# LSTM gates with the batch on the partitions in a merged stage: states as stationary operand in four column groups, weights moving, and a new order of the small work around them

## The reference, cut to what matters

```python
x = x + _L1_ffn_ref(_L1_cond2_ref(x, cond_1024, Wx, Wh, b), ...)      # LSTM, then a 16-expert FFN
... _L2_cond_ref(x, cond_1024, Wx, Wh, b) ...                          # the next layer's LSTM on the new x

def step(carry, xz_t):                       # both LSTMs, 128 steps each, batch 32, width 128
    z = xz_t + prev_h @ Wh                   # xz_t = x_t @ Wx + b, 4 gates x 128
    i, f, o, g = sigmoid(ai), sigmoid(af), sigmoid(ao), tanh(ag)
    next_c = f * prev_c + i * g
    next_h = o * tanh(next_c)

def _L1_ffn_ref(h):                          # per token, all 16 experts are computed, 2 are weighted in
    logits = h @ Wr + br                     # the two best, softmax over them
    u = layernorm(h @ W1[e] + b1[e]); y[e] = gelu(u * g1 + be1) @ W2[e] + b2[e]
    return sum over the two best of weight * y[e]
```

## Time and profile before

| what | value |
|---|---|
| median of 3 runs | 4663.28 us (4662.86 to 4663.63) |
| the profiled execution: its time, its span | 4662.41 us, 4660.6 us |
| PE busy, DVE, ACT, POOL over the span | 92%, 54%, 40%, 16% |
| granted TensorE clock, mean over the span | 0.959 |
| the stage's first and last `gate_tanh` (L1552) | 1433.1 and 2233.3 us |
| one step in the loop, mean of 80 | 5.575 us |

### The profile page before, as it was taken

How to read it: one execution, slowest core, us unless ns; L and a number is a source line. 1 busy time by engine, 2 the same in 40 slices (tenths; PEclk the granted TensorE clock), 3 DMA queues, 4 the chain that set the end, 5 groups by cost and what they waited for, 6 DMA issues and landing times. The chain is left out here.

```text
span 4660.6 us, 118083 instructions
## 1 busy us (share of the span) xinstructions
PE 4309.6 (92%) x41087; PEld 3214.5 (69%) x41087; DVE 2494.8 (54%) x7506; ACT 1859.3 (40%) x4669; POOL 761.1 (16%) x3314
## 2 busy tenths in 40 slices
PE   6999999999998999998799999999997887889998
PEld 4556777777876888886355787787875555566666
DVE  5775664555554777776555444666666563421111
ACT  4433443333331444444233222666664452333333
POOL 1111220000001555554122000111111210000000
PEclk9999999999998999998699998999998997989999
DMA  1000000000000000000000000000000100000000
GB/s 53 0 0 25 0 0 25 0 0 0 0 0 10 1 2 1 1 1 1 33 1 0 3 0 0 3 3 3 3 3 2 52 0 1 0 1 0 0 0 18
DMA packets 3080, 28.73 MB, mean 6 GB/s; under 512 B 320, under 2 KB 832, under 8 KB 1216
## 3 DMA queue, kind: packets, MB, share of 16 engines
q1 hardware_dynamic: 2768, 24.81, 1.4%
HBM read 22.71 MB, written 2.10 MB: 5 GB/s over the span
## 5 line engine op out<-in xcount | busy, mean ns | idle before, releaser
L2231 DVE SCALAR_TENSOR_TENSOR experts_acc<-banks,experts_gate,experts_acc 128x128 f32<-128x128 f32 x512 | 144.2, 345 | 461.7 <-PE banks L2177 460.6
L2177 PEld LDWEIGHTS banks<-weights,experts_hidden 128*128 128x128 f32 x2560 | 303.3, 192 | 55.0 <-issue 49.7
L604 DVE TENSOR_REDUCE cells_row_max<-banks 128x4 f32<-128x512 f32 x384 | 238.5, 684 | 161.6 <-PE banks L397 161.6
L2177 PE MATMUL banks<-weights,experts_hidden 128*128 128x128 f32 x2560 | 305.2, 275 | 0.0
L761 PE MATMUL banks<-clock_fill 128*128 128x512 bf16 x932 | 284.8, 394 | 7.4 <-DVE wave_bias_parts L1612 7.4
L2450 ACT ACTIVATE experts_hidden<-banks,weights 128x512 f32<-128x512 f32 x256 | 175.8, 687 | 268.5 <-PE banks L2447 265.2
L1412 PEld LDWEIGHTS banks<-act_a,weights 128*128 128x128 f32 x2032 | 256.1, 196 | 25.6 <-DVE act_a L1670 18.0
L2447 PE MATMUL banks<-act_a,weights 128*128 (+1 forms) x512 | 262.3, 643 | 0.7 <-ACT experts_hidden L2450 0.3
L1412 PE MATMUL banks<-act_a,weights 128*128 (+1 forms) x2032 | 248.7, 281 | 10.8 <-DVE act_a L1670 10.7
L541 ACT ACTIVATE cells_probs<-banks 128x512 f32<-128x512 f32 x384 | 198.2, 603 | 95.0 <-PE banks L437 90.0
L604 DVE TENSOR_REDUCE attn_row_max<-banks 128x4 f32<-128x512 f32 x256 | 159.0, 684 | 134.8 <-PE banks L397 134.8
(11 more groups left out here) (522 smaller groups left out, 9904.5 us busy)
## 6 DMA issues: line engine op xcount, KB each, us to landing
weights<-in_p SPq DMA_DIRECT2D x1, 2894.5 KB, 17.2
weights<-in_p SPq DMA_DIRECT2D x1, 2894.0 KB, 9.2
weights<-in_p SPq DMA_DIRECT2D x2, 1364.0 KB, 7.1
x_res<-in_x SPq DMA_DIRECT2D x1, 2048.0 KB, 14.9
out_x<-x_res SPq DMA_DIRECT2D x1, 2048.0 KB, 6.3
weights<-in_p SPq DMA_DIRECT2D x1, 1836.0 KB, 10.9
weights<-in_p SPq DMA_DIRECT2D x1, 1835.5 KB, 6.9
weights<-in_p SPq DMA_DIRECT2D x1, 1344.5 KB, 9.8
```

The lines of the kernel that those rows point to most:

```text
L604: dve.tensor_reduce(mt[:, 4 * g:4 * g + 4], bank, AX_X, ALU.max).then_inc(s["max_ready"], 1)
L2177: last = pe.matmul(ps[:, 2 + e % 2, t * P:(t + 1) * P], hs[lo:lo + n, (tile + f) % slots, t * P:(t + 1) * P], out_rhs(e, f, lo, n), start= ...
L2231: last = dve.scalar_tensor_tensor(out=acc[:, t, :], in0=ps[:, 2 + e % 2, t * P:(t + 1) * P], scalar=g[:, t, e:e + 1], in1=acc[:, t, :], op ...
```

## The change

Batch goes on the partitions for the gates. The gates of a step are computed as state (128 channels x 32 sequences, stationary) times weights (moving, 4 gates x 64 channels = 256 columns). Four such matmuls write four groups of 32 partitions: two halves of the channels x two LSTMs (`gates_part`, `lo = 32 * (2 * half + j)`). The same form is used for the inputs (`inputs` on PE, with `Wx`), one step ahead, in place of `pre`. The bias is one matmul in two of four steps. The gate tiles are then 128 partitions x 4 gates x 64 channels, always full width, also where only one LSTM runs.

The next state must be turned back to channels on partitions: `state` on DVE writes two 64x64 blocks of `hb`, `turned` on PE multiplies it with a picking matrix (128x128 stationary, 64 columns moving), and `state` on ACT copies the result into the `ring`, which releases `h_ready`. POOL copies the inputs of four positions to `xq` (`input_quad`), the later LSTM's states from the ring to `core.a` (`keep`); `router_source` is gone, since `logits` reads the ring.

The orders change as well. On POOL `tile_sum` goes to the front of the step, ahead of `newton`; `newton` has 12 operations instead of 13. On DVE `sums` and `guess` come ahead of `units` and `add`, and the routing is cut into single operations at six places of a step (`route(st, known, at)`); the last operation of part 1, `dist`, stands at place 5, behind `add`.

The core of the diff:

```diff
-    RSRC, HSRC, GSRC = 4, 16, 20
-    NEWTON, ROUTING = 12, 15
-    FOLD, FOLD_BIAS = (0, 2, 4, 5), 7
+    STATE, HBANK, TURN, OUT = 2, 4, 6, 7
+    HSRC, GSRC, KEPT = 12, 20, WAVE_LAG + AHEAD
+    NEWTON, ROUTING = 11, 16
+    FOLD, FOLD_BIAS = (3, 7, 4, 5), 3
...
+        th = sb("gates_tanh", [P, 4, HALF])
+        og, c2, fc, ic, tc = (sb(n, [P, HALF]) for n in ("output_gate", "c_twice", "fc", "ic", "tc"))
+        hb = sb("state_by_batch", [P, P])
+        ring = sb("states", [P, 2, WAVE_PERIOD, NB])
+        xq = sb("inputs", [P, 2, 2, AHEAD * NB])
...
+            def input_quad(j, time, parity):
+                xs = positions(core.x, time, AHEAD)
+                pool.tensor_tensor(xq[:, j, parity, :].rearrange("p (t b) -> p t b", t=AHEAD), xs,
+                                   unit_quad, ALU.mult).then_inc(s["x_earlier" if j else "x_later"], 1)
+
+            def inputs(st, known):
+
+                past(pool, s["z_done"], st.s())
+                if not known or st.c + 4 < P:
+                    input_quad(1, st.s(4), (st.c // 4 + 1) % 2)
+                if not known or 0 <= st.c + 4 - WAVE_LAG < P:
+                    pool.wait_ge(s["stored"], st.every4(WAVE_LAG - 4) + 1)
+                    input_quad(0, st.s(4 - WAVE_LAG), (st.c // 4 + 1) % 2)
+
+            def keep(time, m):
+                states = ring[:, 0, 4 * m:4 * m + 4, :]
+                pool.tensor_tensor(positions(core.a, time, AHEAD), states, unit_quad, ALU.mult).then_inc(s["kept"], 1)
...
+                it = item(st, SUM, known)
+                if it is not None and it[2] == 3:
+                    tile_sum(it[0], it[1], (st.c - SUM) // 4 % 2)
+                if st.c % 4 == 0:
+                    inputs(st, known)
+                    if not known or KEPT <= st.c < KEPT + P:
+                        pool.wait_ge(s["h_ready"], st.s())
+                        keep(st.s(-KEPT), (st.c // 4 - 1) % 4)
...
-            def bias(st, j, bank):
-                pe.matmul(ps[:, bank, :], bias_w[0:68, j, :], pick[0:68, :, :, :], start=True, stop=False,
-                          skip_group_check=True)
-
-            def pre(st, known):
-                k, quad = st.c % 4, st.c // 4 + 1
-                for j in range(2):
-                    if known and not 0 <= quad * 4 - WAVE_LAG * (1 - j) < P:
-                        continue
-                    bank = 2 * (quad % 2) + j
-                    if k == 0:
-                        if j == 0:
-                            pe.wait_ge(s["stored"], st.every4(0) + (1 - WAVE_LAG // 4 + 1))
-                            if known and quad * 4 == WAVE_LAG:
-                                pe.wait_ge(s["halved"], 6)
-                                pe.wait_ge(s["bias_ready"], 5)
-                        bias(st, j, bank)
-                    out = ps[:, bank, k * AHEAD * NB:(k + 1) * AHEAD * NB].rearrange("p (t b) -> p t b", t=AHEAD)
-                    pe.matmul(out, packs[j]("Wx", k * P, P), positions(core.x, time_of(st, j, 4 - k), AHEAD),
-                              start=False, stop=False, skip_group_check=True)
+
+            def bias(st, known):
+
+                early = known and st.c + 1 < WAVE_LAG
+                if known and st.c + 1 in (0, WAVE_LAG):
+                    pe.wait_ge(s["halved"], 3 if early else 6)
+                    pe.wait_ge(s["bias_ready"], 4 if early else 5)
+                pe.matmul(ps[:, (st.c + 1) % 2, :], pick[0:68, :], bias_w[0:68, int(early), :].unsqueeze(
+                    1).broadcast_to([68, 2, 4 * HALF]), start=True, stop=False, skip_group_check=True)
...
+            def gates_part(st, j, half, state, name):
+                lo, at = NB * (2 * half + j), st.c // 2 % 2 * 4 * HALF
+                return pe.matmul(ps[lo:lo + NB, st.c % 2, at:at + 4 * HALF].rearrange(
+                    "p (g f) -> p g f", g=4), state, half_of(packs[j], name, half), start=False,
+                    stop=name == "Wh", skip_group_check=True)
...
+                k, parity = st.c % 4, st.c // 4 % 2
+                for half in range(2):
+                    for j in js:
+                        gates_part(st, j, half, xq[:, j, parity, k * NB:(k + 1) * NB], "Wx")
...
             def recurrent(st, known):
-                k, bank = st.c % 4, 2 * (st.c // 4 % 2)
                 past(pe, s["h_ready"], st.s())
-                for j in running(st, known):
-                    first = known and st.c == WAVE_LAG * (1 - j)
-                    state = const("cond").unsqueeze(1) if first else positions(core.a, time_of(st, j, -1))
-                    for z in range(4):
-                        lo = (z * AHEAD + k) * NB
-                        last = pe.matmul(ps[:, bank + j, lo:lo + NB].unsqueeze(1), packs[j]("Wh", z * P, P), state,
-                                         start=False, stop=True, skip_group_check=True)
+                for half in range(2):
+                    for j in running(st, known):
+                        first = known and st.c == WAVE_LAG * (1 - j)
+                        state = const("cond") if first else ring[:, j, (st.c - 1) % WAVE_PERIOD, :]
+                        last = gates_part(st, j, half, state, "Wh")
                 last.then_inc(s["z_done"], 1)
+
+            def turned(st):
+                pe.wait_ge(s["batch_ready"], st.s(1))
+                pe.matmul(ps[:, STATE, 0:2 * NB], hb[:, :], const("half_pick"), start=True, stop=True).then_inc(
+                    s["turned_ready"], 1)
...
             def body(st, known):
                 recurrent(st, known)
+                later = Wave(st.i, st.c + 1)
+                if later.c % 4 < 2:
+                    bias(st, known)
+                if later.c < P + WAVE_LAG:
+                    inputs(later, known)
                 if known:
                     fold(st)
                     fill_ends(st)
                 summed = tile_at(st, TOTAL, known)
                 if summed is not None:
                     total(st, summed)
-                scored, turned = tile_at(st, LOGITS, known), tile_at(st, GTURN, known)
+                scored, gated = tile_at(st, LOGITS, known), tile_at(st, GTURN, known)
                 if scored is not None:
                     logits(st, scored)
-                if turned is not None:
-                    gates_turn(st, turned)
+                if gated is not None:
+                    gates_turn(st, gated)
                 it = item(st, HID, known)
                 if it is not None:
                     hidden(st, *it)
                 it = item(st, OUTPUT, known)
                 if it is not None:
                     output(it[0], it[2], summed)
+                turned(st)
...
+            def state(st, known):
+                if st.c % 4 == 0:
+                    if not known or WAVE_PERIOD <= st.c < P + WAVE_PERIOD:
+                        act.wait_ge(s["source_ready"], st.every4(WAVE_PERIOD) + 1)
+                    if not known or WAVE_LAG + WAVE_PERIOD <= st.c:
+                        act.wait_ge(s["kept"], st.every4(WAVE_LAG + WAVE_PERIOD) + 1)
+                act.wait_ge(s["turned_ready"], st.s(1))
+                act.activation(ring[:, :, st.c % WAVE_PERIOD, :], ps[:, STATE, 0:2 * NB].rearrange(
+                    "p (j b) -> p j b", j=2), ACT.Copy).then_inc(s["h_ready"], 1)
...
             def distance(group):
-                act.wait_ge(s["dist_ready"], group + 1)
+                act.wait_ge(s["route"], group * ROUTING + 12)
...
             def body(st, known):
-                js = running(st, known)
-                lo, hi = js[0], js[-1] + 1
                 group = group_at(st, 2, known)
                 if group is not None:
                     distance(group)
                 it = item(st, OUTPUT, known)
                 if it is not None:
                     gelus(it[0], it[2])
-                gate_tanh(st, lo, hi)
+                gate_tanh(st)
                 tile = tile_at(st, GTURN, known)
                 if tile is not None:
                     gates_kept(st, tile)
-                cell_tanh(st, lo, hi)
+                cell_tanh(st)
                 it = item(st, HID, known)
                 if it is not None:
                     square(it[0], it[2])
+                state(st, known)
...
+            def state(st):
                 dve.wait_ge(s["gate_ready"], st.s(1))
                 dve.wait_ge(s["tc_ready"], st.s(1))
-                out = core.a[:, :].rearrange("p (b t) -> p t b", t=P)[
-                    :, bass.ds(time_of(st, lo), hi - lo, WAVE_LAG), :]
-                dve.tensor_tensor(out, tc[:, lo:hi, :], og[:, lo:hi, :], ALU.mult).then_inc(s["h_ready"], 1)
+                for half in range(2):
+                    rows = slice(half * HALF, (half + 1) * HALF)
+                    last = dve.tensor_tensor(hb[rows, rows], tc[rows, :], og[rows, :], ALU.mult)
+                last.then_inc(s["batch_ready"], 1)
...
             def body(st, known):
-                js = running(st, known)
```

(68 more changed lines are left out.)

222 lines of the change are left out of this document (127 added, 95 removed).

## The result

The changed kernel takes 4709.58 us (median of 4 runs, 4697.58 to 4713.94), the kernel before beside it 4663.45 (4662.86 to 4668.53): ratio 1.0092, 95% interval 1.0071 to 1.0114. It is slower by 46 us, where +55 was forecast. The profiled execution is the fastest of the four, 4697.58 us with a span of 4695.8.

What follows compares the result with a forecast made beforehand. PE bounds the loop before; after it DVE, ACT and PE lie close, with waits for the late add. Ends 20, middle 7, clock 20 and 8 sum to +55 us, 4718 us; range 4620 to 4785.

Steps and rivals of the forecast that it cites:

- The form of the matmuls: On PE, two new sets at 0.48 us each, with form changes, turned and bias: 1.56 in place of 2.58 a step.
- Rival 2: Column groups on PE don't overlap with 256 moving columns: PE's step 6.5 us, time 4813 us; chance 0.03.
- PE's gain lands in idle time: In the loop PE's step falls from 4.99 to about 4.0 us, but DVE's step of 4.40 us becomes the bound.
- tile_sum ahead of newton, and total: Waits on POOL and PE for the late add make two of four steps 6.5 and 5.4 us; four steps 20.7.
- Routing: Single operations on DVE, the late dist and the stall at the loop's pass: 2.2, 2.0 and 3.1 us per 16 steps.
- The clock: PE less busy, a fifth of the time at half speed: +20 us over 130 steps, +8 at the ends.
- the middle: The 130 steps with experts (18 to 147): +7 us from a step of 5.63 against 5.575, +20 from the clock.
- The ends: Thirty steps bound by the chain of a state (0 to 17, 148 to 159): +0.7 us each, +20 in all.
- The sum: Over the whole kernel 20 + 7 + 20 + 8 = +55 us, from 4663 to 4718 us.
- Rival 1: POOL's extra 1.3 us behind tile_sum doesn't reach DVE and the clock stays: step 5.1, time 4622 us; chance 0.26.

Runs made afterwards that it cites:

- hidden_first: The changed kernel with PE's hidden moved ahead of total, logits and gates_turn: 4654.44 us.
- fill_wait: The changed kernel with eight bf16 matmuls of 512 columns that compute nothing put on PE ahead of total: 4670.45 us.
- distance_late: The changed kernel with ACT's distance moved from the head of its step to behind cell_tanh: 4694.48 us.
- ends_no_fill: The changed kernel without the matmuls that compute nothing which PE runs in the first 18 and last 12 steps: 4721.97 us.
- combined: The changed kernel with tile_sum last on POOL, distance behind cell_tanh on ACT, and hidden ahead of total, logits and gates_turn on PE: 4584.82 us.
- sum_last: The changed kernel with tile_sum moved to the end of POOL's step, behind newton, source and tile_gates: 4624.64 us.
- add_early: The changed kernel with DVE's add moved to right behind state, ahead of sums: 4664.58 us.

## Why the prediction was right, step by step

**The form of the matmuls.** Right: 0.46 for a set (0.48 forecast), 0.11 for leaving the form (0.14), `turned` 0.17, or 0.27 after a wait (0.22), PE's step 4.09 (about 4.0). Rival 2 is out.

**PE's gain lands in idle time.** Right: PE's share in the loop is 362.6 / 454.0 = 80%, where 75% was written. Matmuls at half speed count as busy, but that explains little of it: hidden_first, whose clock is 1.00 from 1720 to 1890 us, has 137.7 / 170.0 = 81% there. PE's work of a step was counted a little low (4.2; two passes with little low clock, 1828.13 to 2005.69 us, have 141.2 us of it in 32 steps, 4.4) and the step, 5.63, a little long.

**tile_sum ahead of newton, and total.** Right as a mechanism, and its share was the largest one: taking it back is worth 85 us. In detail the waits are shorter than written. The wait of `units` is 1.4 us, not 2.1, because DVE itself is late there (in the step shown, `units` could have started 3.6 after the end of `add`, not 2.7: `cell` waited 0.61 for `gate_tanh`, and `sums` 0.24 for `square`). And PE's stop at `total` is 2.6 us, not over 3. Four steps took about 20.5 against 20.7, so other parts of them are longer than written.

**Routing.** 2.2 + 2.0 + 3.1 = 7.3 per pass forecast; the best passes are 88.8 = 4 x 20.5 + 6.8, with some 4 round the `dist` and the rest mostly at the loop's turn. Of the 4 some 1.7 is one step at half speed behind the `dist` (6.2 where fill_wait has 4.6 at full clock). Without any low clock, in two passes of fill_wait (88.1 and 87.9), a step is 5.50 (5.63 forecast). What the text missed lies round the `dist`: `logits` and `gates_turn` wait on PE for the `gelus` of the same step, so ACT's late `gelus` holds up `hidden` as well. Before, 1.72 us of `recurrent` covered that the earlier trace rows. hidden_first takes `hidden` out from behind these waits and the one at `total` at once, so it does not tell their shares.

**The clock.** Right in kind, mis-sized in both factors: a fifth of the time at half speed was written, for 0.15 us a step, which is 0.13 us for each us at half speed. In the loop it was 41 of 454 us, and the price was higher: fill_wait is 30.6 us shorter in the middle for 68 us less of the lower level, or 0.45. So +20 was forecast there and 30.6 measured. Half speed came where the text put it, from `total` on, and also behind the `dist`, which it does not name. At the ends +8 was forecast. Steps 0 to 12 and the last twelve ran at full clock, but from step 13 on, behind a stop of PE of 1.95 us, 10 us lay at the lower level (the window of 0.76 above) and two steps took 4.4 and 4.6, which the steps in their place in distance_late did in 3.4 and 3.6: about +2. The kernel before has 5 us at the lower level in its last steps, so next to nothing is left of the term. ends_no_fill shows that without the fills it would have been about 10 more.

**The ends.** +0.78 in an ordinary step (3.36 after 2.58), +0.7 forecast; in sum +22.8 us for +20, the 2 us of low clock included. These steps in the timeline:

```profile
2258.45 0.43 PE L1447 MATMUL banks<-constants,wave_state_by_batch 128*128 128x64 f32 x2
...
2258.98 0.22 ACT L1603 ACTIVATE wave_states<-banks 128x64 f32<-128x64 f32 x1 [1.14 <-PE banks L1447]
2259.25 0.14 PEld L1419 LDWEIGHTS banks<-weights,wave_states 128*32 128x32 f32 x4 [0.51 <-ACT wave_states L1603]
2259.26 0.63 PE L1419 MATMUL banks<-weights,wave_states 128*32 128x256 f32 x4 [0.37 <-ACT wave_states L1603]
2259.93 0.38 ACT L1589 ACTIVATE wave_gates_tanh<-banks 128x256 f32<-128x256 f32 x1 [0.73 <-PE banks L1419]
```

`turned` with its wait and the copy take 0.81 (0.75 forecast), and the four matmuls to `gate_tanh` 0.67.

**The sum.** For the profiled run: ends +22.8 (20 + 8), middle +16.1 (7 + 20), and the start of the stage -5.6, for which the text had under 1. In the runs with the same start the first `gate_tanh` lies anywhere from 1423.9 to 1432.5, in the two with the old one at 1433.1 and 1435.7; whether the new start saves something or this is scatter is open. The median run of the changed kernel is 12 us above the profiled one. I take that for more steps at low clock: the mean granted clock is 0.957 in the profiled run and 0.952 to 0.954 in the three others, though only one of the four has a trace. With it +46 were measured for +55.

The direction and the causes were right, but the closeness of the middle is in part luck, since its two terms were off in opposite directions. The order alone was to make a step 0.055 us longer than before, +7 us; without low clock it is 5.50, some 0.07 shorter, which over 130 steps would be about -10 (an estimate). Half speed was to cost 20 and cost 30.6, in the fastest of the four runs. So it is the low clock, together with the longer ends, that makes the changed kernel slower than the one before; the waits at `tile_sum` and `total` by themselves use up most of PE's gain (combined, which shortens them, has 4.80 us a step in the loop), and they are where PE stood when the clock fell. sum_last, which shortens them, took back both.

Rival 1, the faster one, fell for the reason given: `units` waits for POOL in 22 places. With `tile_sum` at its old place it comes true: sum_last lies at 4624.64, where that rival gave 4622, and its middle is 59.9 us shorter than before, where that rival gave 61.

## What to carry to other kernels

When the engine that bounds is relieved, read the new order of every other queue for pairs in which one engine's last work of a step is another one's first of the next: that pair (`add` and `tile_sum`, `dist` and `distance`) sets the step as soon as the cover is gone. A gap of 2 to 3 us on PE can cost twice, once as a wait and once as matmuls at half speed behind it (for 41 of the 454 us here), so try work that is ready ahead of the wait before anything else. And try such moves together as well as alone: distance_late gave little by itself and all of its 3 us a pass once the larger wait was out, while add_early was good alone and cost 95 us on top of the others.

## What was not expected of the hardware

Four column groups with fp32 operands and 256 moving columns run eight instructions in 0.46 us, where eight on the full array with 128 columns take 0.89. A second surprise was how unevenly one pattern can fall: with the same order, the step with `total` took 6.56, 7.12, 8.7 or 10.0 us in different places of one execution. The first two are both at full clock, and what tells them apart I did not find; in the 8.7 and the 10.0 the granted clock was at its lower level for 3.4 and 6.8 us. Stops of PE of 2.67 and 2.86 us were followed by half speed, one of 1.95 at step 13 too, others of 2.15 and 2.30 were not.
